# Attention phase of an audio tower kernel: work moved between slots, a product rewritten and squares moved from ScalarE to GpSimd

## What is computed

```python
q = _rmsnorm(_rope(q), q_norm_w)
k = _rmsnorm(_rope(k), k_norm_w)
mask = (cols <= rows) & (rows - cols <= WINDOW)
scores = jnp.einsum('bqgtd,bqgsd->bqgts', q, k) * scale
scores = jnp.where(mask[None, None, None], scores, NEG)
attn = jax.nn.softmax(scores, axis=-1)
out = jnp.einsum('bqgts,bqgsd->bqgtd', attn, v)
return out @ wo.T
```

## Time and profile before

| | |
|---|---|
| median of 3 runs | 2319.99 us (2319.36 to 2320.64) |
| the profiled execution | 2317.79 us |
| its span in the profile | 2316.0 us |
| granted clock of PE, mean | 0.976 |
| busy over the span: PE, PEld, DVE, ACT, POOL | 90%, 64%, 73%, 63%, 34% |
| steps on POOL and others that recur in the attention, over the span | normalize 256 x 1041 ns, add_q 128 x 1277 ns |
| first and last minus-maximum product | 1205.67 and 2064.23 us |

### The profile page before, as it was taken

How to read it: one execution, slowest core, us unless ns; L and a number is a source line. 1 busy time by engine, 2 the same in 40 slices (tenths; PEclk the granted TensorE clock), 3 DMA queues, 4 the chain that set the end, 5 groups by cost and what they waited for, 6 DMA issues and landing times. The chain is left out here.

```text
span 2316.0 us, 35857 instructions
## 1 busy us (share of the span) xinstructions
PE 2077.2 (90%) x10589; PEld 1492.2 (64%) x10661; DVE 1682.9 (73%) x3691; ACT 1470.6 (63%) x3736; POOL 777.3 (34%) x1413
## 2 busy tenths in 40 slices
PE   4999999999999977999958888888888888877999
PEld 3788888888888865877735555555555555544554
DVE  4677787787787765566558888888888888864555
ACT  1466656666666643444438888888888888863554
POOL 0111211112112110132256555655556555534100
PEclk9999999999999998999969999999999999997999
DMA  3000000000000000000000000000000000000000
GB/s 111 11 7 7 6 10 6 6 9 6 6 9 6 0 0 1 1 1 1 1 0 1 1 1 1 1 1 1 1 1 1 1 1 1 1 1 3 12 10 14
DMA packets 14447, 15.24 MB, mean 7 GB/s; under 512 B 9995, under 2 KB 10251, under 8 KB 14051
## 3 DMA queue, kind: packets, MB, share of 16 engines
q1 hardware_dynamic: 14307, 13.58, 2.0%
HBM read 11.48 MB, written 2.10 MB: 6 GB/s over the span
## 5 line engine op out<-in xcount | busy, mean ns | idle before, releaser
L1416 ACT ACTIVATE apb<-ps,anb,arq 128x128 f32<-128x128 f32 x1024 | 455.9, 461 | 104.2 <-DVE anb L1290 103.6
L1524 POOL TENSOR_TENSOR apb<-apb,arc 128x512 f32<-128x512 f32 x256 | 266.5, 1041 | 236.5 <-DVE arc L1299 236.5
L1169 PE MATMUL ps<-akT,aqT 128*128 128x256 f32 x1024 | 263.5, 380 | 8.8 <-issue 2.5
L1284 DVE TENSOR_REDUCE amx<-ps 128x4 f32<-128x512 f32 x256 | 175.1, 684 | 97.9 <-PE ps L1169 97.3
L1180 PEld LDWEIGHTS ps<-const,apb 128*128 128x128 f32 x1024 | 112.4, 141 | 178.3 <-issue 106.5
L1416 ACT ACTIVATION_READ_ACCUMULATOR apb<-ps,anb,arq 128x1 f32 x1024 | 211.5, 207 | 0.0
L117 PE MATMUL ps<-h0h,w123h 128*128 128x512 f32 x512 | 207.2, 405 | 3.4 <-POOL h0l L602 1.7
L1169 PEld LDWEIGHTS ps<-akT,aqT 128*128 128x128 f32 x1024 | 196.3, 192 | 21.3
L1518 POOL TENSOR_TENSOR aqr<-at 128x512 f32<-128x512 f32 x128 | 163.4, 1277 | 127.1 <-DVE at L1245 127.1
L119 PE MATMUL ps<-h0h,w123l 128*128 128x512 f32 x512 | 202.8, 396 | 0.0
L1180 PE MATMUL ps<-const,apb 128*128 128x128 f32 x1024 | 162.5, 281 | 44.8 <-POOL apb L1524 43.9
(11 more groups left out here) (303 smaller groups left out, 5317.5 us busy)
## 6 DMA issues: line engine op xcount, KB each, us to landing
x<-in_x SPq DMA_DIRECT2D x32, 176.0 KB
out<-fyo SPq DMA_DIRECT2D x16, 128.0 KB, 1.9
w<-in_w SPq DMA_DIRECT2D x1, 1024.0 KB, 7.8
mw<-in_mw SPq DMA_DIRECT2D x1, 1024.0 KB, 9.6
const<-in_const SPq DMA_DIRECT2D x1, 612.0 KB
wqkv<-in_wqkv SPq DMA_DIRECT2D x1, 576.0 KB, 9.7
fw<-in_fw SPq DMA_DIRECT2D x1, 512.0 KB, 8.3
fsel<-in_fsel SPq DMA_DIRECT2D x1, 512.0 KB, 7.9
```

What stands on the lines that cost most here:

```text
L1169: last = pe.matmul(bank[:, p * 2 * T:(p + 1) * 2 * T], qT[:, i % 2, 2 * k + p, :], kT[:, i // 4 % 2, i % 4, :, :].rearrange("p a s -> p (a ...
L1284: ve.tensor_reduce(mx[:, k, :], ps[:, SB[n % 3], :].rearrange("p (h s) -> p h s", h=4), AX_X, ALU.max).then_inc(S["mx"], 1)
L1416: last = ac.activation(pb[:, i % 2, head, :], ps[:, SB[n % 3], h * T:(h + 1) * T], ACT.Exp, bias=nb[:, k, h:h + 1], scale=rq[:, i % 2, hea ...
L1524: po.tensor_tensor(p, p, rc[:, i % 2, 4 * k:4 * k + 4].unsqueeze(2).to_broadcast([T, 4, T]), ALU.mult).then_inc(S["pn"], 1)
```

## The change

It has five pieces. (1) The two halves of an item's queries are worked on two slots apart (slots 4i-5 and 4i-3 for projection, rope, addition; 4i-3 and 4i-1 for the transposes), so that a rope falls in every odd slot. `rms_q` gets a table of its own (slot 4i-1). (2) On PE `p_v` is the last step of its slot; on DVE `p_copy` comes ahead of `recip`. (3) `k_t`, `w_o` and `turn` move by two, one and one slots; `residual` and `statistics` come one and three slots after `turn`. (4) The reduce for the maximum negates, and the product with `rq` becomes a plain `tensor_tensor`. (5) The squares are taken of the rotated queries `qr` by POOL, behind the addition, instead of by ACT from PSUM; `q_t` no longer waits for them.

```diff
-    at_kt = by_slot(QUADS, lambda q: first(q) + 10)
-    at_q = by_slot(HALVES, lambda m: 4 * (m // 2 - 1) + m % 2)
-    at_qt = by_slot(HALVES, lambda m: 4 * (m // 2 - 1) + 2 + m % 2)
+    at_kt = by_slot(QUADS, lambda q: first(q) + 12)
+    at_q = by_slot(HALVES, lambda m: 4 * (m // 2) - 5 + 2 * (m % 2))
+    at_qt = by_slot(HALVES, lambda m: 4 * (m // 2) - 3 + 2 * (m % 2))
+    at_rms = by_slot(B, lambda i: 4 * i - 1)
     at_pt = by_slot(PARTS, lambda n: n + 2)
     at_pv = by_slot(HALVES, lambda m: 4 * (m // 2) + 4 + 2 * (m % 2))
-    at_wo = {16 * (q + 1) + 3 + c: (q, c) for q in range(QUADS) for c in range(4)}
-    at_tr = by_slot(QUADS, lambda q: 16 * (q + 1) + 8)
-    SLOTS = range(first(0) - 4, max(at_tr) + 2)
+    at_wo = {16 * (q + 1) + 4 + c: (q, c) for q in range(QUADS) for c in range(4)}
+    at_tr = by_slot(QUADS, lambda q: 16 * (q + 1) + 9)
+    SLOTS = range(first(0) - 4, max(at_tr) + 4)
...
                 def q_t(m):
                     h = m % 2
-                    pe.wait_ge(S["sq"], m + 1)
                     pe.wait_ge(S["qr"], m + 1)
...
                     if 0 <= u < PARTS:
                         scores(u)
-                    if u in at_pv:
-                        p_v(at_pv[u])
                     if u in at_pt:
                         p_t(at_pt[u])
...
                     if u in at_tr:
                         turn(at_tr[u])
+                    if u in at_pv:
+                        p_v(at_pv[u])
...
-                    ve.tensor_reduce(mx[:, k, :], ps[:, SB[n % 3], :].rearrange("p (h s) -> p h s", h=4), AX_X, ALU.max
-                                     ).then_inc(S["mx"], 1)
+                    ve.tensor_reduce(mx[:, k, :], ps[:, SB[n % 3], :].rearrange("p (h s) -> p h s", h=4), AX_X, ALU.max,
+                                     negate=True).then_inc(S["mx"], 1)
...
-                    ve.scalar_tensor_tensor(out=nb[:, k, :], in0=mx[:, k, :], scalar=-1.0,
-                                            in1=rq[:, i % 2, 4 * k:4 * k + 4], op0=ALU.mult, op1=ALU.mult
-                                            ).then_inc(S["nb"], 1)
+                    ve.tensor_tensor(nb[:, k, :], mx[:, k, :], rq[:, i % 2, 4 * k:4 * k + 4], ALU.mult
+                                     ).then_inc(S["nb"], 1)
...
                     if 0 <= u < PARTS:
                         maximum(u)
+                    if u in at_pt:
+                        p_copy(at_pt[u])
                     if 0 <= u - 1 < PARTS:
                         recip(u - 1)
-                    if u in at_pt:
-                        p_copy(at_pt[u])
...
-                    if u in at_tr:
-                        residual(at_tr[u])
                     if u - 1 in at_tr:
-                        statistics(at_tr[u - 1])
+                        residual(at_tr[u - 1])
+                    if u - 3 in at_tr:
+                        statistics(at_tr[u - 3])
...
-                def square(m):
-                    i, h = m // 2, m % 2
-                    ac.wait_ge(S["rope"], m + 1)
-                    if i >= 1:
-                        ac.wait_ge(S["ssq"], m - 1)
-                    ac.activation(sqb[:, h, :], ps[:, QB[h], :], ACT.Square).then_inc(S["sq"], 1)
...
-                    if u - 1 in at_q:
-                        square(at_q[u - 1])
                     if u - 1 in at_qt:
                         keep_q(at_qt[u - 1])
-                        if at_qt[u - 1] % 2 == 0:
-                            rms_q(at_qt[u - 1] // 2)
+                    if u in at_rms:
+                        rms_q(at_rms[u])
...
                     if i >= 1:
                         po.wait_ge(S["qt"], m - 1)
+                        po.wait_ge(S["sq"], m - 1)
                     po.tensor_tensor(qr[:, h, :], t1[:, h, :], t2[:, h, :], ALU.add).then_inc(S["qr"], 1)
+
+                def square_q(m):
+                    i, h = m // 2, m % 2
+                    po.wait_ge(S["qr"], m + 1)
+                    if i >= 1:
+                        po.wait_ge(S["ssq"], m - 1)
+                    po.tensor_tensor(sqb[:, h, :], qr[:, h, :], qr[:, h, :], ALU.mult).then_inc(S["sq"], 1)
...
                         normalize(u - 1)
                     if u in at_q:
                         add_q(at_q[u])
+                        square_q(at_q[u])
```

## The result

The changed kernel takes **2387.68 us** (median of 4 runs, 2386.24 to 2392.12) against 2320.31 us for the kernel before beside it (2319.36 to 2321.23): a ratio of 1.0294, 95% interval 1.0276 to 1.0311. It is slower by 2.9%; 2385 was forecast. The profiled execution took 2392.12 us with a span of 2390.3 us.

The account below looks back on a forecast made before the run. Waits, not a full engine, bound the kernel; the new order closes a ring through POOL. 4.2 us more per quad gives 63, last quad and head about 1 each: 65 on 2317.8, 2383, plus 2.2 for the median: 2385 us, range 2325 to 2425.

Parts of the forecast that it names:

- The ring: Attention phase: rope, POOL's addition, square and normalization, PE's transposes, DVE's copy, recip, next rope; 6.38 us per pair of slots.
- The walk pair by pair: Each of a quad's eight slot pairs timed from recip of its odd slot, extras included: 6.74 to 8.9, sum 58.6 us.
- If the square were dearer, all eight pairs would pay: POOL's square at 1.28 instead of 1.04 us would add 8 x 0.24 = 1.9 us per quad.
- The load: Busy time over the same parts: POOL's share up by 98 us, ACT's down by 58.
- The square at 1.04 us: POOL's 128x512 square, not in the trace, taken as the cheap form, like the normalization: 1.04 us.
- The bound of 1.28: Other end for POOL's square: the dear form, priced like the addition, 1.28 us.
- 6.6 us for the ring: Length per pair of slots with the dearer form of the square; the whole kernel some 29 us longer.
- The product: DVE's minus-maximum product slips between two POOL instructions; wanted after 2.88 it ends at 3.94; the plain form gains nothing.
- POOL goes first: Rival: waiting product let in only after the square, 0.7 us in three pairs, some 2.4 per quad: 2421 us; chance 0.06.
- x late: Slots 15 to 1: low part of x ends at 4.62 behind addition and square, delaying x_t; recip at 8.9, ring alone 7.1.
- The sum: Eight pairs make 58.6 us per quad against 54.4: 4.2 more, 63 us over 15 quads; together 65 us.
- The head: Start of attention: queries of item 0 wait for addition, square and sum one after the other; about 1 us.

## Why the prediction was right, point by point

**The ring.** The pairs are where the working put them, from 0.01 to 0.14 us each (table above). That the place of the square makes the loss is shown: doubling it cost 142 us; taking it away from there, onto ACT or behind the normalization, gave back 83 and 66 us. The way on from the square is another matter. The ring of 6.38 us led through normalization, transposes and copy, and the sign given for it, the copy's wait as one of the largest, did not come: 11.1 us, where `sum_q`'s wait for the square is 27.7. The walk pair by pair was better than the ring it started from, because it let residual, statistics and rope_k follow behind sum_q; in the pairs from 9, 11 and 1 that is the way that binds, by the trace. No run cuts this way alone. "If the square were dearer, all eight pairs would pay" was wrong: six did in full, one in part and one not at all.

**The load.** For the same number of parts (188 of them, scaled from 174) POOL's busy time is up by 96 us, 98 forecast, and ACT's down by 46, 58 forecast.

**The square at 1.04 us.** Measured 1039 ns. The bound of 1.28 was too high for two inputs that are the same tensor. So was the estimate of 1.1 us before the dispatch from the Trainium skill (GPSIMD Engine Reference, Elementwise — side-by-side cycle accounting). The prediction's 6.6 us for the ring beside that estimate are worked out with 1.28; with 1.1 they would be 6.4.

**The product.** It slips in between addition and square when it is wanted early enough, and ends with the square when it is late; both forms alike. The rule of the Trainium skill (SBUF — State Buffer, Who interferes with whom) agrees: two SBUF inputs against a POOL instruction that reads SBUF, here a median of 372 and 374 ns for 161 undisturbed. Of the 256 products of the changed kernel 159 were held up, and each ended 0.01 or 0.02 us after the POOL instruction beside it. So the rival "POOL goes first" is out; its price, three times 0.7 us, is 2.1 per quad and not the 2.4 that it gave.

**x late.** Shown by moving it a slot: 38 us. The step "ends at 4.62 behind addition and square" gave 8.9 us for the pair, 8.97 measured.

**The sum.** Forecast 4.2 us per quad and 63 in 15 quads. The 15 steps from slot 1 to slot 1 sum to 876.3 us against 812.5 before, 63.8 more. But this agreement is partly luck: two errors cancel. An undisturbed quad is 58.14, not 58.6, so 3.7 over the 54.41 of before; and the half-speed stretches, which the prediction did not have at all, add some 10 us in the profiled execution (the 13 middle quads sum to 766.3 us, 13 undisturbed ones would be 755.8). That is the term that was missing: I took PE's durations behind a 2.9 us idle time to be those of full speed. (The profiled execution is 4.4 us above the median of its kernel.) Two orders that were priced at nothing were not free either, each tried alone: without "p_v last" the kernel was 12 us faster, without the copy ahead of recip 15, both against the changed kernel run beside them.

**The head** was mis-sized: 1 us forecast, and the first product stands at 1211.94 instead of 1205.67, of which 2.8 us were there before the attention began (POOL's last pooling steps start at 1162.43 for 1159.61). The other 3.5 come from a chain that I did not see. With k_t two slots later the first keys now pass ACT behind rms_q, which waits for the second half's squares:

```profile
1207.16 0.31 ACT L1386 ACTIVATE alrq<-assq,epsc 128x16 f32<-128x16 f32 x1 [4.50 <-DVE assq L1276]
...
1207.62 1.18 ACT L1380 ACTIVATE akT<-ps 64x512 f32<-64x512 f32 x2
...
1208.86 0.61 PE L1166 MATMUL ps<-maskb,identb 128*128 128x512 bf16 x1 [2.40 <-ACT akT L1380]
```

Before, that copy of the keys started at 1198.11. The later k_t alone does not cost it: with the squares on ACT it stands at the same place, and the first product comes 16.1 us after the first x_t, against 18.1 before and 21.6 in the changed kernel. It takes POOL's squares as well, which make rms_q late. The rest of the 74.3 us between the two profiled executions: 1.5 in the last quad, 1.5 behind the last product, 1.2 in the first slot.

**What the change was good for** is real as well, but smaller than the prediction read it. The 1.50 us of the earlier trace rows is the stall of one item in four; before the maxima of the other three items of a quad DVE stood idle for about 1.2, 1.0 and 0.4 us. PE's wait for qT, 24 times and 10.6 us in the steady stretch before, is gone from the list. With the squares elsewhere the new slots are 15 us faster than the old ones, with x in time 1.7% faster.

## What to carry to other kernels

When work moves to an engine with idle time, don't ask how much of it is free: ask what stands behind the new instruction in its in-order queue, and which steps on other engines wait for its result. Walk every way on from it, also the one through the queue of the engine that reads the result (here sum_q on DVE), and see which comes back to the start last. Add it up from rows, one number per link; here the walk gave every pair of slots within 0.15 us, and the ring drawn first was the one that binds in only two of them. And if a fix makes an engine wait for a step that used to be early (x, here), look for all steps that share the queue with the new instruction and move them to slots where it isn't.

## What the runs showed of the hardware

PE's clock fell to half in the middle of a phase in which PE was otherwise 84% busy, after idle times of 2.6 us, and in the run with the later square after 1.5 us. It did not fall each time: with the squares on ACT, PE waited 1.52 us at the same place, and the clock fell behind it in 3 quads and stayed at 1.00 in the others; the changed kernel waited 2.63 us in every quad, and in 6 of 13 nothing followed; with recip first it waited 2.86 us and nothing followed in any. The seven falls of the changed kernel lengthened their quads, counted from slot 9, by 1.4 to 1.8 us each. What decides between the two was not settled: runs of one and the same kernel, the one with the later square, spread over 23 us (2302 to 2325), the shortest with the highest mean clock.
